# First layer's attention on Trainium2: one written plan for the order of units, maxima six units ahead

## What is computed

```python
q = (x @ Wq.T + bq).reshape(b, s, HEADS, HEAD_DIM)
k = (x @ Wk.T + bk).reshape(b, s, HEADS, HEAD_DIM)
v = (x @ Wv.T + bv).reshape(b, s, HEADS, HEAD_DIM)
attn = jnp.einsum('bqhd,bkhd->bhqk', q, k) / np.sqrt(HEAD_DIM).astype(np.float32)
attn = jax.nn.softmax(attn, axis=-1)
attn = attn * head_mask[None, :, None, None]
out = jnp.einsum('bhqk,bkhd->bqhd', attn, v).reshape(b, s, HIDDEN)
return out @ Wo.T + bo
```

## Time and profile before

| | us |
|---|---|
| median of 3 runs (4040.51 to 4053.42) | 4045.18 |
| the profiled execution, its own time | 4054.44 |
| its span | 4053.1 |
| PE busy | 3121.8 (77%) |
| DVE busy | 2586.1 (64%) |
| ACT busy | 2027.6 (50%) |
| POOL busy | 1555.6 (38%) |
| mean granted TensorE clock | 0.836 of full |

### The profile page before, as it was taken

The page is one execution under the profiler, slowest core; times in us unless marked ns, Lnnn a source line. Parts: engine busy times, 40 slices in busy tenths (PEclk is TensorE's granted clock), DMA queues, the critical chain, the costliest instruction groups (busy, mean ns, idle before and its releaser), DMA issues.

```text
span 4053.1 us, 40791 instructions
## 1 busy us (share of the span) xinstructions
PE 3121.8 (77%) x14850; PEld 1366.2 (34%) x14850; DVE 2586.1 (64%) x2891; ACT 2027.6 (50%) x3628; POOL 1555.6 (38%) x938
## 2 busy tenths in 40 slices
PE   5777877975567777777875879766687888888886
PEld 2111212341222222222322643322144554555544
DVE  4676672438998788888877234487726655555553
ACT  1454453124456766666565221567444555555654
POOL 2211100113457666666757002244414444444432
PEclk6788897986678878877777879888698998999998
DMA  3111200011111121121111001000000000000000
GB/s 86 38 36 26 43 7 2 0 55 48 35 35 36 31 56 35 35 51 40 33 24 44 10 0 64 21 21 21 21 0 19 19 19 10 19 19 10 19 10 31
DMA packets 79733, 114.60 MB, mean 28 GB/s; under 512 B 16270, under 2 KB 49422, under 8 KB 78106
## 3 DMA queue, kind: packets, MB, share of 16 engines
q1 hardware_dynamic: 68268, 103.33, 10.5%
q0 software_dynamic: 11264, 8.66, 1.6%
HBM read 37.96 MB, written 17.33 MB: 14 GB/s over the span
## 4 chain that ended last, share of the span: by engine, by line
PE 50%; DVE 21%; ACT 16%; issue 6%; POOL 3%; DMA 2%; SPq 1%; POOLq 0%; DVEq 0%; ACTq 0%
DVE layer_mamba_state L1335 7%; DVE psum L1323 4%; PE psum L1107 3%; PE psum L774 3%; PE psum L2455 3%; PE psum L1184 3%; ACT layer_mamba_decay L1261 3%; PE psum L2486 3%; ACT layer_exps L787 2%; PE psum L238 2%; PE psum L2149 2%; PE psum L226 2%; PE psum L900 2%; PE psum L232 2%; PE psum L822 2%
## 5 line engine op out<-in xcount | busy, mean ns | idle before, releaser
L1364 POOL TENSOR_TENSOR layer_mamba_state<-layer_mamba_state,layer_mamba_c 128x1024 f32<-128x1024 f32 x320 | 780.4, 2448 | 597.1 <-DVE layer_mamba_state L1335 588.6
L1335 DVE TENSOR_TENSOR_SCAN layer_mamba_state<-layer_mamba_decay,psum 128x1024 f32<-128x1024 f32 x320 | 731.5, 2286 | 43.7 <-ACT layer_mamba_decay L1261 11.5
L1184 PE MATMUL psum<-layer_mamba_state,two_to_one 128*64 128x512 f32 x1280 | 443.7, 785 | 121.1 <-DVE layer_mamba_x L1352 77.0
L1261 ACT ACTIVATE layer_mamba_decay<-layer_mamba_delta_wide,layer_weights 128x511 f32<-128x511 f32 x640 | 415.6, 711 | 74.5 <-DMA layer_mamba_delta_wide<-layer_mamba_delta 38.2
L1323 DVE TENSOR_TENSOR psum<-psum,layer_mamba_u_wide 128x1024 f32<-128x1024 f32 x320 | 393.4, 1229 | 62.9 <-PE psum L1142 26.2
L714 DVE TENSOR_REDUCE layer_peak<-psum 128x2 f32<-128x1024 f32 x256 | 308.7, 1222 | 123.0 <-PE psum L685 118.4
L787 ACT ACTIVATE layer_exps<-psum 128x1024 f32<-128x1024 f32 x256 | 249.8, 1030 | 223.2 <-PE psum L754 223.2
L2852 POOL TENSOR_TENSOR layer_p<-layer_p,layer_stats 128x512 f32<-128x512 f32 x128 | 133.0, 1040 | 294.5 <-DVE layer_stats L2775 294.4
L2646 ACT ACTIVATE layer_p<-psum,layer_stats 128x128 f32<-128x128 f32 x512 | 181.2, 369 | 127.9 <-DVE layer_stats L2768 126.3
L1142 PE MATMUL psum<-layer_mamba_bc,layer_mamba_pick 96*64 96x512 bf16 x768 | 165.1, 457 | 91.2 <-DVE psum L1323 67.5
L2839 POOL TENSOR_TENSOR layer_qk<-layer_qk,layer_v_between 128x1024 f32<-128x1024 f32 x64 | 150.4, 2350 | 217.7 <-DVE layer_v_between L2739 215.9
(11 more groups left out here) (349 smaller groups left out, 6257.2 us busy)
## 6 DMA issues: line engine op xcount, KB each, us to landing
layer_mamba_delta_wide<-layer_mamba_delta SPq DMA_DIRECT2D x160, 128.0 KB, 2.3
layer_mamba_u_wide<-layer_mamba_work SPq DMA_DIRECT2D x160, 128.0 KB, 2.4
layer_v_between<-layer_v SPq DMA_DIRECT2D x16, 512.0 KB, 4.3
qk_dram<-layer_qk_parts SPq DMA_DIRECT2D x16, 384.0 KB, 2.6
layer_q_rows<-qk_dram SPq DMA_DIRECT2D x96, 64.0 KB
layer_k_rows<-qk_dram SPq DMA_DIRECT2D x96, 64.0 KB
layer_v_between<-layer_v SPq DMA_DIRECT2D x16, 384.0 KB, 5.6
layer_weights<-weights_dram SPq DMA_DIRECT2D x1, 4147.0 KB, 12.3
```

Of the source, the lines that this page charges most:

```text
L1184: e = pe.matmul(c.psum[j * HALF:(j + 1) * HALF, self.sum_banks[h], :], c.two_to_one[:, :], self.state[i % len(self.state)][:, j, :], start ...
L1261: e = act.activation(decay[:, j, 1:SEQ], self.delta_wide[h][:, j, 1:SEQ], ACT.Exp, scale=rates[:, rate:rate + 1])
L1335: dve.tensor_tensor_scan(state, decay, self.fill.rearrange("p j t -> p (j t)"), 0.0, ALU.mult, ALU.add).then_inc(self.scanned, 1)
L1364: pool.tensor_tensor(state, state, self.both(self.c_wide[turn % self.C_BUFFERS][:, :]), ALU.mult).then_inc(self.multiplied, 1)
```

## The change

- All stages carry planned times (in units of one step): attend(b) starts at 32b + 0.1, divide(b) at 32(b+1) + 1, maxima(b) at 32(b-1) - 6 + 0.2, project(b) at 32(b-2) + 0.3 (project(0) at -46, project(1) at -38). Each further step of a stage is planned 1.0 later, and every engine takes steps in the order of their times.
- So in round b, PE has after W14 and W15 of attend(b-1): A0, M6, P0 | S, A1, M7 | D0, A2, M8, P1 | D1, A3, M9 | D2, W0, A4, M10 | D3, A5, M11 | O, W1, A6, M12, V | ... | A25, M31 | W11, A26, T, M0' | A27, M1' | ... | A31, M5' | W14, W15. The M are of maxima(b+1), the M' of maxima(b+2). Divide stands one step later than before.
- In the opening, P0 of project(1) stands in front of M0 of maxima(0) rather than behind it, and M0 to M5 of maxima(1) stand between M31 of maxima(0) and A0 of attend(0).
- `next_pair` gives the pairs of banks in PE's own order, counted modulo 3, instead of by the two formulas.
- No instruction of computation or DMA is added or taken away.

```diff
+def paced(run, first):
+
+    time = first
+    while True:
+        yield time
+        if next(run, "over") == "over":
+            return
+        time += 1.0
...
+    LEAD = 6
...
-        self.pair_read = {}
+        self.pair, self.pair_read = {}, {}
         self.pool_setup()
         self.sp_setup()
-        weave(self.run(self.pe_project, self.pe_maxima, self.pe_attend, self.pe_divide))
+        play(self.run(self.pe_project, self.pe_maxima, self.pe_attend, self.pe_divide))
...
-        def on(stage, b):
-            if 0 <= b < SEQS:
-                yield from stage(b)
-
-        weave(on(project, 0))
-        weave(on(maxima, 0), on(project, 1))
-        for b in range(SEQS + 1):
-            weave(on(divide, b - 1), on(attend, b), on(maxima, b + 1), on(project, b + 2))
-        yield
-
-    def maxima_pair(self, b, i):
-
-        return 2 * ((i + 1 if b == 0 else UNITS0 + 2 * UNITS0 * (b - 1) + 2 * i + 2) % 3)
-
-    def attend_pair(self, b, i):
-        last = b == SEQS - 1
-        return 2 * ((UNITS0 + 2 * UNITS0 * b + (i + 1 if last else 2 * i + 1)) % 3)
+        runs, opening = [], -UNITS0 - self.LEAD
+        for b in range(SEQS):
+            runs += [paced(divide(b), UNITS0 * (b + 1) + 1), paced(attend(b), UNITS0 * b + 0.1),
+                     paced(maxima(b), UNITS0 * (b - 1) - self.LEAD + 0.2),
+                     paced(project(b), (opening - 8, opening)[b] if b < 2 else UNITS0 * (b - 2) + 0.3)]
+        return merged(*runs)
+
+    def next_pair(self, unit):
+
+        self.pair[unit] = at = 2 * (len(self.pair) % 3)
+        if at in self.pair_read:
+            self.c.pe_hold.wait_ge(*self.pair_read[at])
+        return at
...
-            at = self.maxima_pair(b, i)
             hold.wait_ge(self.rows_ready[s], self.rows_loaded(b))
-            if at in self.pair_read:
-                hold.wait_ge(*self.pair_read[at])
+            at = self.next_pair(("maxima", b, i))
...
-            at, g = self.attend_pair(b, i), 2 * quad + half
+            at, g = self.next_pair(("attend", b, i)), 2 * quad + half
...
-            hold.wait_ge(*self.pair_read[at])
```

More of the change, by code:

```diff
@@ L544, in __init__ @@
         self.peak_ready = [signal(f"peak_ready{s}") for s in range(SLOTS0)]
-        self.pair_read = {}
+        self.pair, self.pair_read = {}, {}
         self.pool_setup()
         self.sp_setup()
-        weave(self.run(self.pe_project, self.pe_maxima, self.pe_attend, self.pe_divide))
[L549 to L554, removed]
+        play(self.run(self.pe_project, self.pe_maxima, self.pe_attend, self.pe_divide))
+        play(self.run(self.act_project, self.act_maxima, self.act_attend, self.act_divide))
+        play(self.run(self.dve_project, self.dve_maxima, self.dve_attend, self.dve_divide))
+        play(self.run(self.pool_project, self.pool_maxima, self.nothing, self.nothing))
+        play(self.run(self.sp_project, self.sp_maxima, self.nothing, self.nothing))
     def nothing(self, b):
@@ L711, in dve_maxima @@
             block, g = divmod(i, PAIRS0)
-            at = self.maxima_pair(b, i)
+            at = self.pair["maxima", b, i]
             hold.wait_ge(self.peaks_scored, UNITS0 * b + i + 1)
@@ L782, in act_attend @@
         for i in range(UNITS0):
-            at = self.attend_pair(b, i)
+            at = self.pair["attend", b, i]
             hold.wait_ge(self.scored, UNITS0 * b + i + 1)
```

## The result

The median fell from 4043.4 us (4039.23 to 4053.42, six runs) to 4026.4 us (4023.31 to 4031.42, six runs): a ratio of 0.9952, interval 0.9939 to 0.9965, 17.0 us less. The forecast was 4023. The profiled execution of the kernel after took 4031.42 us, its span was 4030.1.

The account below looks back on a forecast made before the run. Bound: a three-engine loop of 2.83 us a turn, a gap chained over four engines, a half-clock opening. Four rounds at 2.1 us, one at 11.0, plus 1.3 and 1.0 sum to 21.7 saved: 4023 us, range 3986 to 4040.

Parts of the forecast that it names:

- A0's wait: Gap after W15: with six units of lead A0 waits 1.05 us for its rows, not 9.5.
- the reciprocal in the open: Ahead of D0: the reciprocal, 3.35 us, is no longer hidden; PE idles about 3.0 us and D0 comes 10.4 after W15.
- The steady part, and T at no cost: Steady turns stay 2.83 us; T's 0.60 us fits the 0.68 of PE idle, costing at most 0.60 a round if not.
- The clock from D0 on: D0 to V: clock falls in most rounds since D of 16 rows seems not to count as load; 25.0 us.
- one round at full clock: Of the five rounds with a P1, one keeps full clock from D0 on and saves 11.0 us.
- S at full clock in all rounds: S, between W15 and D0, was counted at its full-clock 3.59 us.
- the clock falls before S: Rival: waits at A0 and P0's bank put P0 and S at half clock, 1.0 and 3.6 us more; 4062, chance 0.07.
- S slower than 3.6: Sign of being wrong in the trace after the change: S taking more than 3.6 us.
- Rounds 6 and 7: Last two rounds: D0 8.6 us after W15, then 17.7 after A26; 1.3 and 1.0 us saved.
- The shorter end: Round 6 ends with six units of A alone, but this mostly turns into A0 of round 7 waiting for the maxima.
- The opening of the stage: Before the first A0: six M hidden in a 9.00 us wait; P0 gains or loses up to 2.08; taken as 0.
- Row loads: M0' needs project's rows at step 26: cost 0, cover at least 7 us; rival of late rows 4055, chance 0.03.

## Why the prediction came out right, and where it didn't

The forecast of the time held, and so did the mechanism in its main line: A0's wait almost gone, the reciprocal in the open, half clock from D0 to O. Two terms of the sum were mis-sized. The steps it names, with what they measured:

- *The steady part, and T at no cost.* Right. 36.3 us for the forecast 36.4; the turn with T is 2.83. In the turn behind it TensorE waits 0.41 us for a maximum, out of the same 0.68 of cover. On ACT, less_peak began at 232.81, 1.35 us after A26's start, forecast 1.45.
- *A0's wait.* 0.71 us in round 2, forecast 1.05. The chain from less_peak to A0 took 8.77 us (232.81 to 241.58) for 8.93.
- *The reciprocal in the open.* Right: 2.90 us ahead of D0 for 3.0. D0 came 10.4 us after W15 in rounds 4 and 5, as forecast, and 12.0 in round 2.
- *The clock from D0 on.* The reason given was that D doesn't count as load; the kernels with 128 rows bear it out as far as two row counts can, and the wait ahead of D0 has its part beside it. D0 to V's end was 24.7 and 24.8 us in rounds 4 and 5, forecast 25.0, O 5.1 to 5.6 for 5.9. The Trainium skill, page "TensorE: Matmul & The Clock Gate", Part 1, has activity release the throttle; the trace agrees where D has 128 rows and the clock is back within P1, but in the window of round 4 above TensorE is busy 23.90 of 24.68 us at a granted clock of 0.59.
- *The sum, first mis-sized term: one round at full clock.* It was put at 11.0 us; none of the five was at full clock from D0 on. At 2.1 like the others, the sum would have been 8.9 less: 12.8 instead of 21.7. The stage gave 14.2. The mistake was to count on a lucky round where each round has both causes of a fall, 16 rows and 2.9 us of idle.
- *Second: S at full clock in all rounds.* The rival "the clock falls before S" came half true, in three rounds of five; "S slower than 3.6" was one of the prediction's own signs of being wrong. But the rival was mis-sized. It was priced at 3.6 us for an S at half clock throughout, plus 1.0 for P0; S lost 1.7, since the clock came back inside it, P0 none, and D0 then ran at 1.12 us instead of 2.07, which gave some of it back. So a falling clock made these rounds hardly slower than the rest: 71.8, 71.7, 71.7 against 71.3, 71.5. A round saved 2.3 us, forecast 2.1.
- *Rounds 6 and 7.* 1.8 us saved up to the last O, forecast 2.3. D0 of round 6 came 8.4 us after W15 (8.6 forecast); in round 7 it came 18.8 us after A26 (582.68 to 601.50), forecast 17.7. TensorE's timeline there:

```profile
592.74 0.61 PE L759 MATMUL psum<-layer_q_rows,layer_k_rows 51*128 51x512 bf16 x2 [2.49 <-DMA layer_q_rows<-peak_dram]
593.28 4.78 PE L819 MATMUL psum<-layer_heads,layer_weights 128*16 128x512 f32 x8
```

  The shorter end became a wait, as forecast; that S behind it would begin at half clock was left out, 1.2 us.
- *The opening of the stage.* 0.8 us saved, forecast 0; A0 waits 5.37 us at the first round instead of 9.00. The stage is counted from its first M, which began 0.9 us later in this profile; a delay of that M isn't in it.
- *Row loads.* No M behind the first waited for its rows; the rival is out.

By parts: 11.6 for five rounds, 1.8 and 0.8: 14.2 us. The forecast of 21.7 was too high by 7.5, and the median came within 4 us of it because 2.8 us more fell off the median than off the profiled stage, and the median of before was 1.8 lower than the one I took. That agreement is no merit of the sum, and whether those 2.8 us are more than chance I can't settle: the comparisons of the two kernels give 17 and 20 us, and profiles spread by 27 us there.

## What to carry to other kernels

When a chain over several engines stands between two passes, measure it in units of the loop that could hide it (8.8 us are a little over six units of 1.4), give a unit or two more (six left a wait of 0.8 us, eight none), and list what the gap was hiding, for that is what one pays next: here a reciprocal of 3.35 us and a block at half clock, worth another 1%. Spread such a block only after its pieces fit into the idle of their engine, and cut the instruction that doesn't. Try padding matmuls of few rows to 128 where the clock falls among them: here the duration at full clock was the same, and the clock came back.

## What the runs showed that I had not expected

- The rows of D made a difference to the clock though not to its time at full clock. 16 or 128 rows take 1.12 us there; with 16, D goes on at 2.07 us until O; with 128, the clock is back within P1 in four rounds of five. Padding the rows brings the ratio to the kernel before from 0.9950 to 0.9853, about 1%, some 39 us, and the stage from 601.5 to 561.9. S has 128 rows but 16 columns of weights, and the clock came back while it ran (5.27 us; at half clock throughout it would be 7.2, twice 3.59).
- The clock fell in S with no long idle before it: 0.71 and 0.87 us, and 1.7 us between them with A, M and P0. The length of the waits doesn't tell the rounds apart: in the same kernel waits of 0.77 and 0.87 us (round 4) left S at 3.59, when it was run again so did 1.07 and 0.87 (round 3), and with 128 rows in D S was fast in four rounds of five with 0.80 to 1.11 and 0.87. What does tell them apart I can't say; no run varied it alone. With no wait at A0, in the kernel of lead eight, it fell before S in none.
- The reciprocal took 3.35 us for 16x512 and 0.88 to 0.95 for 16x128, so its time is nearly in proportion to the columns: four pieces cost 0.4 us more than one.
